# Second attention of a fused block: 64-row score tiles in head pairs, PSUM shared out anew

## The reference

```python
def _L0_attn_b_ref(x, wq, w_down, wk_up, wv_up, wo):   # 16 heads, head size 8, T = 256
    q = (x @ wq).reshape(B, T, H, D)
    lat = x @ w_down
    k = (lat @ wk_up).reshape(B, T, H, D)
    v = (lat @ wv_up).reshape(B, T, H, D)
    q = _apply_rope(q, cos, sin)
    k = _apply_rope(k, cos, sin)
    scores = jnp.einsum('bqhd,bkhd->bhqk', q, k) * scale
    pages = jnp.arange(T) // PAGE_SIZE                     # pages of 32
    allowed = pages[None, :] <= pages[:, None]
    scores = jnp.where(allowed[None, None], scores, jnp.finfo(scores.dtype).min)
    attn = jax.nn.softmax(scores, axis=-1)
    out = jnp.einsum('bhqk,bkhd->bqhd', attn, v).reshape(B, T, E)
    return out @ wo
```

## Time and profile before

| | us |
|---|---|
| median of 3 runs | 582.98 (582.77 to 583.08) |
| span of the profiled execution, first to last instruction | 579.5 |
| outside that span, by the median | 3.5 |
| first transposes of round -1 | 294.7 |
| one round of the hardware loop of the second attention | 19.06 |
| last output sums of the second attention | 472.8 |

### The profile page before, as it was taken

How to read it: one execution, slowest core, us unless ns; L and a number is a source line. 1 busy time by engine, 2 the same in 40 slices (tenths; PEclk the granted TensorE clock), 3 DMA queues, 4 the chain that set the end, 5 groups by cost and what they waited for, 6 DMA issues and landing times.

```text
span 579.5 us, 14261 instructions
## 1 busy us (share of the span) xinstructions
PE 435.6 (75%) x4663; PEld 328.6 (57%) x4679; DVE 340.7 (59%) x1067; ACT 219.0 (38%) x507; POOL 203.6 (35%) x300
## 2 busy tenths in 40 slices
PE   3667899999976299982656899899878862999900
PEld 2545677777765167771334667666666652677700
DVE  4545567677876544444865675667777674455412
ACT  1445655556450022220133667656655410122200
POOL 5032333344453300007865156435712442000054
PEclk9978999999995599995557999999999975899965
DMA  8999200000000011111100000000000001111123
GB/s 262 358 344 292 61 3 3 10 10 9 9 12 16 29 42 52 54 41 41 36 1 2 1 2 2 1 0 0 1 1 6 24 24 32 38 55 54 42 67 91
DMA packets 40895, 30.89 MB, mean 53 GB/s; under 512 B 3344, under 2 KB 37008, under 8 KB 40592
## 3 DMA queue, kind: packets, MB, share of 16 engines
q1 hardware_dynamic: 32176, 23.06, 12.9%
q0 software_dynamic: 2048, 4.20, 2.4%
q10 hardware_dynamic: 6624, 3.02, 1.8%
HBM read 15.26 MB, written 15.01 MB: 52 GB/s over the span
## 4 chain that ended last, share of the span: by engine, by line
PE 54%; DVE 18%; issue 8%; ACT 7%; POOL 6%; DMA 4%; SPq 1%; ACTq 0%; DVEq 0%; another core or an unknown queue 0%; POOLq 0%
PE S L1324 8%; PE bank L1337 7%; PE S L1248 5%; POOL yg L1052 4%; PE S L1330 4%; DVE nmax L497 3%; ACT E L918 3%; PE bank L1203 3%; PE S L1414 2%; PE bank L1367 2%; PE S L1415 2%; PE bank L1427 2%; PE bank L1164 2%; PE bank L1390 2%; PE bank L1225 2%
## 5 line engine op out<-in xcount | busy, mean ns | idle before, releaser
L836 ACT ACTIVATE E<-S,nmax 128x256 f32<-128x256 f32 x128 | 58.9, 472 | 67.9 <-DVE nmax L497 67.9
L1052 POOL DMA_INDIRECT yg<-slots,pos x32 | 30.8, 963 | 140.6 <-DMA slots<-yo 132.1
L1248 PE MATMUL S<-QT,KT 128*128 128x256 f32 x256 | 67.2, 408 | 0.8 <-DVE Va L386 0.5
L880 ACT ACTIVATE hT<-S 128x512 f32<-128x512 f32 x46 | 27.5, 597 | 105.9 <-PE S L1330 105.9
L1013 POOL TENSOR_TENSOR vs<-Va,rden 128x512 f32<-128x512 f32 x32 | 33.3, 1041 | 88.5 <-DVE rden L526 72.3
L497 DVE TENSOR_REDUCE nmax<-S 128x4 f32<-128x1024 f32 x32 | 39.1, 1221 | 31.2 <-PE S L1248 30.6
L918 ACT ACTIVATE E<-S 128x1536 f32<-128x1536 f32 x32 | 46.4, 1450 | 25.4 <-PE S L1418 25.4
L1248 PEld LDWEIGHTS S<-QT,KT 128*128 128x128 f32 x256 | 49.1, 202 | 9.2 <-DVE Va L386 0.6
L1324 PE MATMUL S<-W,xgT 128*128 x92 | 52.3, 652 | 0.0
L684 DVE TENSOR_REDUCE nm<-bank 128x2 f32<-128x512 f32 x64 | 41.1, 683 | 15.7 <-remote 10.6
L1337 PE MATMUL bank<-W,hT 128*128 x368 | 48.5, 275 | 0.0
(11 more groups left out here) (171 smaller groups left out, 1011.1 us busy)
## 6 DMA issues: line engine op xcount, KB each, us to landing
slots<-zeros SPq DMA_DIRECT2D x1, 8640.0 KB, 37.9
xg<-slots SPq DMA_DIRECT2D x46, 64.0 KB, 1.7
slots<-yo ACTq DMA_DIRECT2D x46, 64.0 KB, 1.6
W<-in_L_ffn_W SPq DMA_DIRECT2D x1, 2048.0 KB, 10.0
b<-in_L_ffn_b SPq DMA_DIRECT2D x1, 2048.0 KB, 20.3
x<-in_L_attn_a_x SPq DMA_DIRECT2D x4, 256.0 KB, 3.6
yg<-in_select SPq DMA_DIRECT2D x1, 1024.0 KB, 7.6
out<-x SPq DMA_DIRECT2D x8, 128.0 KB, 2.2
```

What stands on the lines that cost most here:

```text
L836: last = act.activation(E[:, hp, h, c, :], S[hp % 2][:, h, c * T:(c + 1) * T], ACT.Exp, bias=nmax[:, hp, k:k + 1], accum_out=den[:, hp, k: ...
L1052: pool.indirect_dma_start(out=yg[:, t, :], out_offset=None, in_=xs_dram, in_offset=bass.IndirectOffsetOnAxis(pos[:, t:t + 1], 0)).then_inc ...
L1248: last = pe.matmul(S[hp % 2][:, h, c * T:(c + 1) * T], KT[:, p, h, hp, 4 * c:4 * c + 4, :], QT[:, p, :, hp * RT:(hp + 1) * RT], start=True ...
```

## The change

The keys lose their zero halves: `kT` holds the transposed keys as they are, two heads on 128 partitions, and one engine copies all 128 rows (VectorE the first half of the heads, ScalarE the second). A head's scores are now a product over its own 64 rows, and the matmuls of the two heads of a pair are issued one after the other, on rows 0 to 63 and 64 to 127, into two different banks. The same holds for `sel` and `mT`: the parts of the maxima of even heads lie from row 0, those of odd heads from row 64, and `sel` has 8 entries instead of 16.

PSUM is shared out anew. All four banks of `S4` take transposed scores, one head each with 384 columns. The natural scores go by pair of heads (n = 0 to 7) instead of by step of four: a pair's 2 x 384 columns fill the two banks of `M2`. One reduction takes all of it, 768 values into 2 x 3 maxima, and once per batch an elementwise min joins the two maxima of the later queries. `b_scores` waits for the reduction of the pair before (`bs["max"]`), GpSimd waits for `bs["least"]`. The steps stand in a new order in `b_round` of TensorE and VectorE. The clearing of `KT` on GpSimd, half of the load of the selector and two of its casts on ScalarE go.

```diff
         kT = KT[:, 0, :, :, :, :].rearrange("p h s j i -> p (h s j i)").bitcast(BF16).rearrange(
+            "p (a n t) -> p a n t", a=2, t=T)
...
+        pb = [ctx.enter_context(nc.psum_tensor(f"bank{i}", [P, 512], F32)) for i in range(2)]
+        M2 = ctx.enter_context(nc.psum_tensor("M2", [P, 2, 512], F32))
+        pb += [M2[:, i, :] for i in range(2)]
...
-            def b_max(b, q):
+            def b_max(b, n):
...
+                dve.wait_ge(bs["s"], b * 8 + n + 1)
+                dve.tensor_reduce(nm[:, :, :, n].rearrange("p c h -> p h c"),
+                                  M2[:, :, 0:TRI].rearrange("p h (c k) -> p h c k", k=P),
                                   AX.X, ALU.max, negate=True).then_inc(bs["max"], 1)
+                if n == 7:
+                    dve.wait_ge(bs["max"], b * 8 + 8)
+                    dve.tensor_tensor(nm[:, 1, :, :], nm[:, 1, :, :], nm[:, 2, :, :], ALU.min).then_inc(bs["least"], 1)
...
-                if n: b_max(b + 1, 0)
-                if n: b_max(b + 1, 1)
-                if n: b_kT(b + 1, 1 - p, 1)
+                if n:
+                    for k in range(4): b_max(b + 1, k)
...
-                act.activation(Eb[:, q % 2, :, :], S4[:, 0:3, :], ACT.Exp, scale=SCALE_B).then_inc(bs["exp"], 1)
+                act.activation(Eb[:, q % 2, :, :], S4[:, :, 0:TRI], ACT.Exp, scale=SCALE_B).then_inc(bs["exp"], 1)
...
-            pool.wait_ge(a_scores, 4 * B)
-            pool.memset(KT[:, :, :, :, :, :], 0.0).then_inc(bs["zero"], 1)
...
+                waits(pe, bs["max"], b * 8 + n)
+                for h in range(2):
+                    rows = slice(64 * h, 64 * h + 64)
+                    pe.matmul(M2[:, h, P:TRI], qT[rows, p, n, P:T], kT[rows, p, n, :], start=True, stop=True)
+                for h in range(2):
+                    rows = slice(64 * h, 64 * h + 64)
+                    last = pe.matmul(M2[:, h, 0:P], qT[rows, p, n, 0:P], kT[rows, p, n, 0:P], start=True, stop=True)
                 last.then_inc(bs["s"], 1)
...
+                    n = 2 * q + d
+                    for lo, hi, keys, u in ((0, T, slice(0, P), 0), (T, TRI, slice(P, T), 1)):
+                        for h in range(2):
+                            rows = slice(64 * h, 64 * h + 64)
+                            pe.matmul(S4[:, 2 * d + h, lo:hi], kT[rows, p, n, keys], qT[rows, p, n, u * P:T],
+                                      start=True, stop=False)
+                        for h in range(2):
+                            rows = slice(64 * h, 64 * h + 64)
+                            last = pe.matmul(S4[:, 2 * d + h, lo:hi], sel[rows, n, :], mT[rows, u:2, :],
+                                             start=False, stop=True)
...
+                if n: b_scores(b + 1, 1 - p, 7)
+                if c:
                     pe.wait_ge(bs["ot"], b * 4 + 3)
```

More of the change, by code:

```diff
@@ L217, in build @@
         bs = {k: sem(f"b_{k}") for k in
-              ("const", "chain0", "zero", "xb", "p1", "latT", "turnq", "p2", "turnk", "v", "vb", "chain", "split", "rep", "tq", "qT", "tk",
+              ("const", "chain0", "least", "xb", "p1", "latT", "turnq", "p2", "turnk", "v", "vb", "chain", "split", "rep", "tq", "qT", "tk",
                "kT", "kTa", "s", "max", "mchain", "ms", "mt", "mT", "st", "exp", "pv", "ot", "on", "rsum", "att",
@@ L228, in build @@
         block = ctx.enter_context(nc.Block())
-        copies = [(sel[:, 4 * k:4 * k + 4, :], yg[:, 4 * k:4 * k + 4, :]) for k in range(4)]
+        copies = [(sel[:, 4 * k:4 * k + 4, :], yg[:, 4 * k:4 * k + 4, :]) for k in range(2)]
         for t, name in ((qs, "qmask"), (ks, "kmask")):
@@ L911, in b_kT @@
                 act.wait_ge(bs["tk"], b * 2 + i + 1)
[L912 to L913 removed]
+                src = pb[0][:, :].bitcast(BF16).rearrange("p (n t) -> p n t", n=4)
+                act.copy(kT[:, p, 4 * i:4 * i + 4, :], src).then_inc(bs["kTa"], 1)
             def b_exp(b, q):
@@ L1088, in b_maxima @@
                 chain.restart(b * 4)
[L1089 removed]
+                pool.wait_ge(bs["least"], b + 1)
                 waits(pool, bs["mt"], b)
[L1091 removed]
+                parts = ms[:, :, :].rearrange("p u (h r) -> p u h r", h=2)[:, :, :, 0:3 * HB // 2].rearrange(
+                    "p u h (n k) -> p u h n k", k=3)
+                both = nm[:, 0:2, :, :]
                 chain.link(pool.tensor_tensor(
[L1093 to L1096 removed]
+                    parts[:, :, :, :, 0], both,
+                    zeros[:, 0:2 * HB].rearrange("p (u h n) -> p u h n", u=2, h=2), ALU.add))
+                chain.inc(pool.tensor_tensor(nmr[:, :, :, :], both, parts[:, :, :, :, 0], ALU.subtract))
+                chain.link(pool.tensor_tensor(parts[:, :, :, :, 1], both, parts[:, :, :, :, 0], ALU.subtract))
+                chain.link(pool.tensor_tensor(parts[:, :, :, :, 2], nmr[:, :, :, :], parts[:, :, :, :, 1],
+                                              ALU.subtract))
                 pool.sem_inc(bs["ms"], 1)
@@ L1379, in b_tk, with b_scores @@
                 b_transpose(ks, p, i, bs["tk"])
-            def b_scores(b, p, q):
-                if q % 2 == 0:
-                    pe.wait_ge(bs["qT"], b * 2 + 1 + q // 2)
-                    kT_there(b, q // 2)
-                before = (b * 4 + q) * 3 - 2
-                for d in range(2):
-                    n = 2 * q + d
-                    waits(pe, bs["max"], before + d)
-                    pe.matmul(pb[2 + d][:, :], qT[:, p, n, P:T], kT[:, p, n, :, :], start=True, stop=True
-                              ).then_inc(bs["s"], 1)
-                waits(pe, bs["max"], before + 2)
-                for d in range(2):
-                    n = 2 * q + d
-                    last = pe.matmul(S4[:, 3, d * T:(d + 1) * T], qT[:, p, n, 0:P], kT[:, p, n, :, 0:P],
-                                     start=True, stop=True)
+            def b_scores(b, p, n):
+                if n % 4 == 0:
+                    pe.wait_ge(bs["qT"], b * 2 + 1 + n // 4)
+                    kT_there(b, n // 4)
+                waits(pe, bs["max"], b * 8 + n)
[5 more added lines that the diff above has]
+                    last = pe.matmul(M2[:, h, 0:P], qT[rows, p, n, 0:P], kT[rows, p, n, 0:P], start=True, stop=True)
                 last.then_inc(bs["s"], 1)
             def kT_there(b, i):
-                pe.wait_ge(bs["kT"], b * 2 + i + 1)
-                pe.wait_ge(bs["kTa"], b * 2 + i + 1)
+                pe.wait_ge(bs[("kT", "kTa")[i]], b + 1)
             def b_scoresT(b, p, q):
@@ L1410, in b_scoresT @@
                 for d in range(2):
-                    for h in range(2):
-                        n, hh = 2 * q + d, 4 * q + 2 * d + h
-                        dst = S4[:, d, h * T:(h + 1) * T]
-                        pe.matmul(dst, kT[:, p, n, h, 0:P], qT[:, p, n, :], start=True, stop=False)
-                        pe.matmul(dst, sel[:, hh, :], mT[:, :, :], start=False, stop=True)
-                        dst = S4[:, 2, (2 * d + h) * P:(2 * d + h + 1) * P]
-                        pe.matmul(dst, kT[:, p, n, h, P:T], qT[:, p, n, P:T], start=True, stop=False)
-                        last = pe.matmul(dst, sel[:, hh, :], mT[:, 1, :], start=False, stop=True)
+                    n = 2 * q + d
[8 more added lines that the diff above has]
+                                             start=False, stop=True)
                 last.then_inc(bs["st"], 1)
@@ L1590, in _select @@
 def _select():
-    s = np.zeros((P, HB, P), np.float32)
-    for h in range(HB):
-        s[3 * h:3 * h + 3, h, :] = 1.0
-    return s.reshape(P, HB * P)
+    s = np.zeros((P, HB // 2, P), np.float32)
+    for n in range(HB // 2):
+        for h in range(2):
+            s[64 * h + 3 * n:64 * h + 3 * n + 3, n, :] = 1.0
+    return s.reshape(P, HB // 2 * P)
 CST, NCST = {}, 0
```

64 lines of the change are left out of this document (26 added, 38 removed).

## The result

The changed kernel takes 621.22 us (median of four runs, 619.46 to 622.64) against 582.88 of the kernel before (580.87 to 583.08): a ratio of 1.0661, 95% interval 1.0625 to 1.0696. It is slower, as forecast, but by 38.3 us and not by 22; 621.2 lies above the range of 590 to 619. Single executions far above the others of their kernel, the farthest one of 873.24 us among twelve with fillers in round 7, are left out of the ratios in this document, while medians and ranges keep them.

What follows compares the result with a forecast made beforehand. No engine stands alone as the bound: waits alternate between TensorE and ScalarE's exp, with TensorE at work almost throughout. 583 + 12.6 at full clock + 10 for the clock = 605.6, forecast 605, range 590 to 619.

Steps and rivals of the forecast that it cites:

- The walk through a round: One loop round of the second attention, followed step by step on the engines: 20.8 us, 1.75 more than before.
- Overlap of the tiles: In the second attention's scores, a 64-row pair costs one stream instead of two, taking 3.95 us a round off TensorE.
- rival 2: Score pairs don't overlap: loop rounds of 23.8 us, 620 us in all, more with the clock; chance 0.10.
- The sum at full clock: Second attention, loop, rounds -1, 0, 5 and 6, and 7: 7.0 + 3 + 2.8 + 1.3 - 1.5 = +12.6 us.
- What the clock adds: Rounds -1 to 5: TensorE falls to 1.2 GHz about once a round, losing up to 1.7 us each, about 10 us.
- The 3.5 us outside the trace: Median run time less traced span, 583.0 - 579.5; taken as unchanged, so additions to the trace add to the median.
- Rival 1: The clock stays up, as waits under 2.1 us don't bring it down: 595.6 us; chance 0.23.
- Rival 3: Faster: at each pair's wait for the reduction before, TensorE finds enough else or it turns round sooner; 566 us; chance 0.11.

Runs made afterwards that it cites:

- fillers: Changed kernel plus 18 extra bf16 matmuls, results thrown away, before the keys' projection and 18 before the transposes of the maxima; 602.88 us, ratio 1.0329 against the kernel before.
- three further changes: Changed kernel with pairs 5, 7 and repeats earlier, maxima reduced by single heads, transposes of the maxima behind the next round's first transposes; 588.6 us, ratio 1.0049.
- best version: Kernel with reordering, single-head maxima and moved transposes of the maxima, plus 12 extra matmuls behind each transposed step of round 7; 583.88 us, ratio 0.9969.
- the filler there: Kernel with 12 extra matmuls behind each transposed step of round 7, plus 8 before each of pairs 1 to 7 in round -1; 586.34 us, ratio 1.0046.
- pair 7 alone: Changed kernel with one edit, pair 7 ahead of the transposed scores of step 3 instead of behind them; 607.51 us, ratio 1.0411.
- the new order: Changed kernel with pair 5 behind the queries' projection, repeats ahead of reductions 4 and 5, pair 7 ahead of transposed step 3; 592.77 us, ratio 1.0146.
- single heads: Reordered kernel with each M2 bank reduced and waited for by itself, 16 reductions of 384 values per batch; 594.16 us, ratio 1.0172; 588.6 us with transposes moved too.

## Why the prediction was right on the direction and wrong on the size

**The walk through a round: right.** Times from the round's origin:

| | walk | measured |
|---|---|---|
| pair 1 | 3.00 | 2.97 |
| pair 2 | 4.37 | 4.37 |
| pair 3 | 5.76 | 5.77 |
| transposed scores 2 | 7.05 | 7.03 |
| values 1 | 9.2 | 9.44 |
| pair 5 | 9.98 | 10.23 |
| projection of the keys | 12.97 | 13.31 |
| pair 7 | 15.5 | 17.97 |
| transposes of the maxima | 18.37 | 21.02 |

Up to the projection of the keys no step is off by more than 0.34 us. The waits stand where the walk put them: the three turns of M2, the turned queries, and GpSimd's chain at the end (388.43 less 387.11, where the min ends: 1.3 us, as taken from the earlier trace rows). From there on the clock is at half, and from the start of the projection, over values 2 and transposed step 3, to pair 7 it takes 4.66 us instead of 2.5. That is 2.1 of the 2.65 us by which this round is longer than the walk.

**Overlap of the tiles: right.** A transposed step takes 0.67 us against 1.33 in the earlier trace rows; rival 2, no overlap, is out. A change of tile shape costs about 0.09 us again.

**The sum at full clock: nearly right in the loop, too small around it.** With the clock held up by fillers the loop is 8.4 us longer than before, where 7.0 was forecast. Round 0 is 2.7 us longer, forecast 2.8. Rounds 5 and 6 are 4.2 us longer there, at full rate too (42.2 us at 1.00). About 0.8 of it are the fillers themselves, which have no wait for a projection to fill in these rounds: values 2 start 1.38 us after pair 6 with them, and 1.00 without, at the same rate. That leaves 3.4 where 1.3 was forecast, so this term of the order was nearly three times too small. Rounds 7 and 8 are 2.2 us longer instead of 1.5 shorter, but at a clock of 0.76. Round -1 is 6.6 us longer with fillers and 5.1 without, forecast 3; it now runs wholly at 1.2 GHz (0.50 against 0.70 before).

**"What the clock adds": the step that failed.** It gave 10 us over six rounds, from half a 3.4 us stretch lost once a round. That a fall would come, and where in the round, was right. Three things were wrong in the size. The loop spent 30.4 us at 1.2 GHz (95.1 x 0.32), 7.6 a round and not 3.4. No row showed that a fall costs one such stretch: the earlier trace rows end at 313.60, and the trace of before goes on at half rate.

```profile
313.60:317.00 3.40, 2.91 (x22) 2.53 (x23) 0.68 (x1) 1.44 (x2) 3.32 (x6) 0.51 0.00 0
```

The term also stopped at round 5, and counted six rounds where -1 to 5 are seven. But round 6 has the waits of round 5, and rounds 7 and 8 have no pairs and half the streaming in their transposed scores: the clock is 0.75 and 0.69 in these two stages. And round -1, of which 10.2 us were at half rate anyway (17.0 x 0.60), became wholly slow. I reckoned with some 20 us more at 1.2 GHz; it was 90. The price of a microsecond at 1.2 GHz, though, was less than the 0.5 that I took: in the loop 30.4 us of it lie between 85.1 us with fillers and 95.1 without, so 0.33 each; a reduction lasts 0.96 us at either rate (385.95), so the waits for other engines do not stretch with it. The same comparison, with the 0.8 us of fillers taken off, gives 4.4 us for 22.9 in rounds 5 and 6, 1.2 for 5.9 in round 0 and 1.7 for 5.1 in rounds 7 and 8: with the loop 17.3 us for 64.3, 0.27 each. At that rate the 90 us are about 24 us, an estimate, where the sum had 10, and about 15 of the 39.1 remain for the order at full clock, where it had 12.6. So of the 16 us that the forecast fell short, the clock is by far the larger part, some 14 against 2. What was measured directly is less: the fillers alone take back 18 to 19 us (ratio 1.0329 for 1.0661).

The 3.5 us outside the trace, taken as unchanged, did not stay: in the changed kernel the median less the span is 0.5 us, and the profiled execution's own time less its span is 1.9.

**Rival 1**, the clock stays up, fell as a forecast, and the fillers made it true in the loop: 595.6 was its time, 602.88 came, with the clock still down at both ends. **Rival 3**, faster, named the right place. With the turn of M2 halved and the order mended, the loop does come under its "19.1 us or less a round" (18.3), but that takes three further changes, and of the 17 us of gain that it promised a tenth part is there at most: 0.3% in the best version.

**What stays open.** Why round -1 stays 3.7 us or more above the kernel before in the versions that keep the whole maximum: the eight turns of M2 with little between them are in its path, and the clock is at half in it; the two were not told apart, and the filler there disturbs what it should show. Which of the waits in rounds 5 to 8 brings the clock down was not tried singly. That pair 7 alone does not keep the clock up in the loop is shown (0.88 against 0.98); whether pair 5 with the repeats would alone was not run, and which length of gap decides is not shown. Nor were the fillers or the new order tried on the kernel before, so that what they give by themselves is not known.

## What to carry to other kernels

Tiling that halves the streaming on TensorE was worth nothing here, where each group of matmuls waits for the reader of its PSUM buffer: walk the round from buffer turn to buffer turn, and put the producers of a chain over VectorE and GpSimd ahead of the work that is to hide it. Where TensorE's work is thinned out while the round keeps its length, price the clock as a term of its own, in every stage and for the stretches behind each wait, and not as one short loss per round. If fillers make a kernel faster, try the order next: two pairs and the repeats moved were worth 28 us here, the fillers 18.

## What the runs showed of the hardware beyond this

- The two 64-row tiles overlap completely when issued in turn: 16 matmuls of 64 rows in 0.67 us, against 1.33 for as many columns over the full array.
- They overlap by about half when the heads are issued one after the other (1.02 us), because TensorE starts matmuls for the idle rows ahead of queued ones. The same shows in round -1 with single heads: a matmul of pair 7 starts at 312.01, the last of the keys' projection, queued ahead of it, at 312.43.
- A reduction of 384 values takes 0.55 us whether it gives 3 maxima or 6 (549 and 558 ns), of 768 values 0.957, so two small ones cost 0.14 us more than a large one. VectorE's busy time in the loop rose with them from 50.3 to 53.9 us, and this cost nothing there.
- The clock fell in rounds whose longest single wait of TensorE was under 2 us (1.34 and 1.37 us in the round shown), and did not fall in the loop of before, whose idle times stay under a microsecond. In the loop of the new order, with one wait of 1.22 us a round, it stayed up but for 3.4 us in 77.7.
